# Second layer of the experts computed transposed, with the weights stationary and 496 tokens moving

## The reference, cut to what matters

```python
B, L, D = h.shape                                  # 1, 12500, 256
C = max(1, math.ceil(CAPACITY_FACTOR * T / E))     # tokens that an expert takes
buf = jnp.zeros((E, C, D), dtype=h.dtype).at[idx, pos_safe].set(x, mode='drop')
hmid = jax.nn.relu(jnp.einsum('ecd,edf->ecf', buf, w1) + b1[:, None, :])   # 256 -> 1024
ybuf = jnp.einsum('ecf,efd->ecd', hmid, w2) + b2[:, None, :]               # 1024 -> 256
y_tok = ybuf[idx, pos_g] * (prb * kept)[:, None]
y = jnp.nan_to_num(y_tok.reshape(B, L, D), nan=0.0, posinf=10000.0, neginf=-10000.0)
```

## Time and profile before

| | |
|---|---|
| median of three runs | 1618.15 us |
| the profiled execution's own time | 1620.16 us |
| its span, first to last instruction | 1618.4 us |
| TensorE busy | 1425.0 us (88%) |
| DVE busy | 1194.5 us (74%) |
| ACT busy | 929.4 us (57%) |
| POOL busy | 685.3 us (42%) |
| mean granted TensorE clock | 0.941 of full speed |

### The profile page before, as it was taken

How to read it: one execution, slowest core, us unless ns; L and a number is a source line. 1 busy time by engine, 2 the same in 40 slices (tenths; PEclk the granted TensorE clock), 3 DMA queues, 4 the chain that set the end, 5 groups by cost and what they waited for, 6 DMA issues and landing times. The chain is left out here.

```text
span 1618.4 us, 30409 instructions
## 1 busy us (share of the span) xinstructions
PE 1425.0 (88%) x8833; PEld 1261.1 (78%) x8833; DVE 1194.5 (74%) x3087; ACT 929.4 (57%) x1980; POOL 685.3 (42%) x598
## 2 busy tenths in 40 slices
PE   5999999994877777777747999999999999999995
PEld 5999999983655556566536999999999999999994
DVE  5888888874778878878754677776777677777864
ACT  3555555541445645645555676767667676766762
POOL 0000000006556556656624355455455545465434
PEclk8999999996889898989867999999999999999998
DMA  2434434422433443443611121121313112121000
GB/s 78 83 82 82 83 84 84 84 63 70 91 83 85 107 90 81 99 102 81 162 45 50 55 73 20 32 77 47 93 35 99 33 47 78 46 77 41 17 14 18
DMA packets 109592, 112.12 MB, mean 69 GB/s; under 512 B 66311, under 2 KB 89113, under 8 KB 109422
## 3 DMA queue, kind: packets, MB, share of 16 engines
q1 hardware_dynamic: 56682, 72.73, 18.1%
q0 software_dynamic: 52864, 38.82, 11.5%
HBM read 76.17 MB, written 43.85 MB: 74 GB/s over the span
## 5 line engine op out<-in xcount | busy, mean ns | idle before, releaser
L1534 DVE TENSOR_TENSOR h_lo<-q_all,h_hi 128x496 fp32r<-128x496 f32 x256 | 173.4, 677 | 197.9 <-PE psY L1595 89.1
L1332 POOL DMA_INDIRECT out<-q_all,to_i x128 | 176.1, 1376 | 327.9 <-issue 293.2
L1410 ACT ACTIVATE h_hi<-psH,b_sb 128x496 fp32r<-128x496 f32 x256 | 172.6, 674 | 233.4 <-PE psH L1618 225.7
L1595 PE MATMUL psY<-w_hi,h_hi 128*124 128x256 f32 x1024 | 289.3, 283 | 0.0
L1595 PE MATMUL psY<-w_hi,h_lo 128*124 128x256 f32 x1024 | 287.0, 280 | 0.0
L1595 PE MATMUL psY<-w_lo,h_hi 128*124 128x256 f32 x1024 | 286.7, 280 | 0.0
L748 POOL DMA_INDIRECT gl<-alpha_l_table,isrc x100 | 130.5, 1305 | 174.3 <-issue 133.6
L1595 PEld LDWEIGHTS psY<-w_lo,h_hi 128*124 128x124 f32 x1024 | 188.9, 184 | 8.9
L1595 PEld LDWEIGHTS psY<-w_hi,h_hi 128*124 128x124 f32 x1024 | 188.7, 184 | 7.9
L1595 PEld LDWEIGHTS psY<-w_hi,h_lo 128*124 128x124 f32 x1024 | 189.1, 185 | 0.0
L1319 POOL DMA_INDIRECT q_all<-out,from_i x112 | 164.7, 1471 | 54.7 <-issue 54.7
(11 more groups left out here) (230 smaller groups left out, 3338.4 us busy)
## 6 DMA issues: line engine op xcount, KB each, us to landing
x_sb<-in_x SPq DMA_DIRECT2D x50, 448.0 KB
q_all<-in_L_ffn_w SPq DMA_DIRECT2D x16, 1024.0 KB
graph_table<-tab_sb SPq DMA_DIRECT2D x25, 511.0 KB
out<-xd SPq DMA_DIRECT2D x25, 448.0 KB
x_sb<-in_x SPq DMA_DIRECT2D x50, 52.0 KB
out<-q_all,to_i POOLq DMA_INDIRECT x128
q_all<-out,from_i POOLq DMA_INDIRECT x112
gl<-alpha_l_table,isrc POOLq DMA_INDIRECT x100
```

The lines of the kernel that those rows point to most:

```text
L1332: pool.indirect_dma_start(out=out, in_=o_sb[:, par, j, :], in_offset=None, out_offset=bass.IndirectOffsetOnAxis(ap=to_i[:, par, j:j + 1], ...
L1410: act.activation(h_hi[:, f % 4, :], psH[f % 2][:, 0:TS3], ACT.Relu, bias=b1_sb[:, bass.ds(e * NF + f, 1)]).then_inc(s_hhi_ready, 1)
L1534: nc.vector.tensor_tensor(h_lo[:, f % 4, :], hf[:, f % 4, :], h_hi[:, f % 4, :].bitcast(F32), ALU.subtract).then_inc(s_hlo_ready, 1)
L1595: ins = nc.tensor.matmul(psY[par][j // 2][0:T3, (j % 2) * D:(j % 2 + 1) * D], hh[:, f % 4, j * T3:(j + 1) * T3], w[:, f, :], start=f == 0 ...
```

## The change

`second` is turned round. The stationary operand is a 128 by 128 block of `w2`, the moving one is all 496 tokens of `h_hi` or `h_lo`: three passes by two halves of the output channels, 6 matmuls in the place of 12. The result now has channels on partitions and tokens in the free dimension. So

- `with_bias` adds a bias per partition (128 partitions by 496, two instructions as before) and writes `y_t`; `b2` is loaded as rows and turned together with `b1`, in the place of a copy on all partitions;
- a new step of TensorE, `back`, turns `y_t` with eight transposes into `psX`, in step 3 of the next tile, between the first layer's matmuls and `second`; it waits for both of `with_bias`'s instructions;
- `times_prob` reads `psX` and moves from steps 2 and 3 to steps 3 and 5;
- the transposes of step 6, which write the same `psX`, wait for the end of `times_prob`;
- on DVE `limits` and `finite` move from steps 4 and 5 to 6 and 7, and `keep_finite` and `sums` from steps 6 and 7 to steps 0 and 1 of the tile after, ahead of `with_bias`;
- at the end, `keep_finite` and `sums` of the last tile but one, and a last `back`, stand in the closing sequence.

```diff
@@ -699,15 +699,15 @@
-                    b2_end, b1_end = w2_end + E * D, w2_end + E * D + P
+                    bias_end = w2_end + P
...
-                    split_dma(sp, q_all[:, 0, w2_end:b2_end].rearrange("p (a n) -> p a n", a=1),
-                              b2.rearrange("(a e) d -> a (e d)", a=1).partition_broadcast(T3), T3, s_first_in)
-                    sp.dma_start(q_all[0:E * NF, 0, b2_end:b1_end], b1.rearrange("e (c p) -> (e c) p", p=P))\
+                    sp.dma_start(q_all[0:E * NF, 0, w2_end:bias_end], b1.rearrange("e (c p) -> (e c) p", p=P))\
...
+                    sp.dma_start(q_all[E * NF:E * NF + E * KC, 0, w2_end:bias_end],
+                                 b2.rearrange("e (c p) -> (e c) p", p=P)).then_inc(s_first_in, 16)
...
@@ -1194,9 +1194,9 @@
-            b2_bc = carve(T3, E, D)
-            b1_rows = carve(E * NF, P)
-            b1_sb = sb3("b1_sb", [P, E * NF])
+            NBIAS = E * NF + E * KC
+            bias_rows = carve(NBIAS, P)
+            bias_t = sb3("bias_t", [P, NBIAS])
@@ -1210,7 +1210,7 @@
-            yb = carve(T3, J, D)
+            y_t = carve(P, KC, TS3)
...
@@ -1282,6 +1283,9 @@
+
+            def has_two_before(e, st):
+                return not (isinstance(e, int) and e == 0 and st < 2)
@@ -1391,9 +1395,11 @@
                         act.wait_ge(s_fin_done, n - 1)
-                    act.wait_ge(s_yb_done, 2 * (n - 1) + pair + 1)
+                    act.wait_ge(s_y_back, 2 * (n - 1) + pair + 1)
+                    passed(act, s_act_passed)
                     for j in range(2 * pair, 2 * pair + 2):
-                        ins = act.activation(ys[:, j, :], yb[:, j, :], ACT.Copy, scale=prob[:, bass.ds(J * (n - 1) + j, 1)])
+                        ins = act.activation(ys[:, j, :], psX[pair][0:T3, (j % 2) * D:(j % 2 + 1) * D], ACT.Copy,
+                                             scale=prob[:, bass.ds(J * (n - 1) + j, 1)])
                     ins.then_inc(s_ys_done, 1)
@@ -1408,15 +1414,15 @@
                             act.activation(h_hi[:, f % 4, :], psH[f % 2][:, 0:TS3], ACT.Relu,
-                                           bias=b1_sb[:, bass.ds(e * NF + f, 1)]).then_inc(s_hhi_ready, 1)
+                                           bias=bias_t[:, bass.ds(e * NF + f, 1)]).then_inc(s_hhi_ready, 1)
                             act.activation(hf[:, f % 4, :], psH[f % 2][:, 0:TS3], ACT.Relu,
-                                           bias=b1_sb[:, bass.ds(e * NF + f, 1)]).then_inc(s_hf_ready, 1)
+                                           bias=bias_t[:, bass.ds(e * NF + f, 1)]).then_inc(s_hf_ready, 1)
                             if is_first(e, st):
...
                                 root(g + 1)
-                            if f in (2, 3) and not is_first(e, st):
-                                times_prob(g, f - 2)
+                            if f in (3, 5) and not is_first(e, st):
+                                times_prob(g, (f - 3) // 2)
                             if f == 4 and not end:
@@ -1510,13 +1516,12 @@
                 def with_bias(n, par, e):
 
-                    dve.wait_ge(s_ys_done, 2 * (n - 1))
+                    dve.wait_ge(s_y_back, 2 * (n - 1))
                     dve.wait_ge(s_w2_mm, NF * n)
-                    for pair in range(2):
-                        nc.vector.tensor_tensor(yb[:, 2 * pair:2 * pair + 2, :],
-                                                psY[par][pair][0:T3, :].rearrange("p (j d) -> p j d", j=2),
-                                                b2_bc[:, bass.ds(e, 1), :].broadcast_to([T3, 2, D]),
-                                                ALU.add).then_inc(s_yb_done, 1)
+                    for c in range(KC):
+                        nc.vector.tensor_tensor(y_t[:, c, :], psY[par][c][:, 0:TS3],
+                                                bias_t[:, bass.ds(KC * e + E * NF + c, 1)].broadcast_to([P, TS3]),
+                                                ALU.add).then_inc(s_yt_ready, 1)
 
                 def body(e, last):
@@ -1539,16 +1544,16 @@
                             if f == 1 and not end:
                                 scales(g + 1)
-                            if f == 4 and after:
-                                limits(g)
-                            if f == 5 and after:
-                                finite(g)
+                            if f == 0 and has_two_before(e, st):
+                                keep_finite(g - 1)
+                            if f == 1 and has_two_before(e, st):
+                                sums(g - 1, par, (st - 2) % ST, e * (ST // 2) + (st - 2) // 2)
                             if f == 6 and not end:
                                 low_t(g + 1, 1 - par)
                             if f == 6 and after:
-                                keep_finite(g)
+                                limits(g)
                             if f == 7 and after:
-                                sums(g, 1 - par, (st - 1) % ST, e * (ST // 2) + (st - 1) // 2)
+                                finite(g)
                             if st == ST - 1 and not last:
                                 split_w1(f, e + 2)
@@ -1557,6 +1562,8 @@
                 over_experts(dve, body)
+                keep_finite(NG - 1)
+                sums(NG - 1, 0, ST - 2, NG // 2 - 1)
                 with_bias(NG, 1, E - 1)
@@ -1569,33 +1576,43 @@
                     pe.wait_ge(s_hit, KC * g)
                     pe.wait_ge(s_lot, KC * g)
+                    if not (isinstance(g, int) and g < 2):
+                        pe.wait_ge(s_ys_done, 2 * (g - 1))
                     for c in range(KC):
                         for j in range(J):
...
                     ins.then_inc(s_t_done, 1)
 
-                pe.wait_ge(s_first_in, 80)
-                nc.tensor.transpose(psY[0][0][:, 0:E * NF], b1_rows[:, :], ident[0:E * NF, 0:E * NF]).then_inc(s_b1_t, 1)
+                pe.wait_ge(s_first_in, 64)
+                nc.tensor.transpose(psY[0][0][:, 0:NBIAS], bias_rows[:, :], ident[0:NBIAS, 0:NBIAS]).then_inc(s_b1_t, 1)
                 transposes(0)
                 pe.wait_ge(s_b1_set, 1)
 
+                def back(n):
+
+                    pe.wait_ge(s_yt_ready, KC * n)
+                    for pair in range(2):
+                        for j in range(2 * pair, 2 * pair + 2):
+                            for c in range(KC):
+                                ins = nc.tensor.transpose(psX[pair][0:T3, (j % 2) * D + c * P:(j % 2) * D + (c + 1) * P],
+                                                          y_t[:, c, j * T3:(j + 1) * T3], ident[:, :])
+                        ins.then_inc(s_y_back, 1)
+
                 def second(e, st, f):
 
                     g, par = ST * e + st, st % 2
                     if f == 0 and not (isinstance(e, int) and e == 0 and st < 2):
-                        pe.wait_ge(s_yb_done, 2 * (g - 1))
+                        pe.wait_ge(s_yt_ready, KC * (g - 1))
                     if st == 0:
                         pe.wait_ge(s_w2hi, NF * e + f + 1)
...
                     pe.wait_ge(s_hhi_ready, NF * g + f + 1)
                     pe.wait_ge(s_hlo_ready, NF * g + f + 1)
-                    for j in range(J):
-                        for n, (hh, w) in enumerate(((h_hi, w2_hi), (h_hi, w2_lo), (h_lo, w2_hi))):
-                            ins = nc.tensor.matmul(psY[par][j // 2][0:T3, (j % 2) * D:(j % 2 + 1) * D],
-                                                   hh[:, f % 4, j * T3:(j + 1) * T3], w[:, f, :],
-                                                   start=f == 0 and n == 0 and j % 2 == 0,
-                                                   stop=f == NF - 1 and n == 2 and j % 2 == 1)
+                    for n, (w, hh) in enumerate(((w2_hi, h_hi), (w2_lo, h_hi), (w2_hi, h_lo))):
+                        for c in range(KC):
+                            ins = nc.tensor.matmul(psY[par][c][:, 0:TS3], w[:, f, c * P:(c + 1) * P], hh[:, f % 4, :],
+                                                   start=f == 0 and n == 0, stop=f == NF - 1 and n == 2)
                     ins.then_inc(s_w2_mm, 1)
 
@@ -1621,6 +1638,8 @@
                                 transposes(g + 1)
+                            if f == 3 and not is_first(e, st):
+                                back(g)
                             if f >= 2:
@@ -1629,6 +1648,7 @@
                 for f in range(NF - 2, NF):
                     second(E - 1, ST - 1, f)
+                back(NG)
 
         late.close()
 

```

13 lines of the change are left out of this document (7 added, 6 removed).

## The result

The changed kernel takes 1679.07 us, the median of four runs (1674.64 to 1681.53); the kernel before took 1617.85 us beside it (1615.28 to 1619.96). The ratio is 1.0376, with a 95% interval of 1.0349 to 1.0403: slower by 61 us, where 67 were forecast. The profiled execution took 1674.64 us, its span is 1672.6 us.

The account below looks back on a forecast made before the run. TensorE, without idle time at full clock, was taken as the bound. -18 + 24.8 + 44 + 11.5 + 3.4 = 66 us on the profiled 1620.16 gave 1686, 1684 against the median, written as 1685 us; range 1665 to 1710.

Parts of the forecast that it names:

- Parts 1 and 2: TensorE's queue: six matmuls of `second` for twelve save 18 us; `back`'s eight transposes add 24.8 us in 31 tiles.
- part 1: `second` on TensorE takes 1.34 us for 1.41, 0.07 us less, 256 times: 18 us saved.
- Part 3: `back` on TensorE waits for DVE's `with_bias`, 1.0, 1.7 or 2.5 us in 29 tiles: together 44 us.
- Part 4: Step 6's transposes wait for ACT's `times_prob`: 0.24 us in 23 tiles, 0.86 in 7; together 11.5 us.
- Part 5: Closing sequence: `with_bias` comes 1.9 us later on DVE, ACT then starts 1.5 us later; sum 3.4 us.
- at nothing: Priced at zero: `with_bias` itself, loads of `b2`, POOL's gathers (rows used over a tile later), the later limits.
- The queue alone: Rival: both new waits of TensorE are met in time, only its queue and the end count; 1628 us, chance 0.09.
- The not slower case: Rival: `back`'s transposes cost half of 0.77 us per block, waits are met; 1615 or 1616 us, chance 0.03.
- The clock rival: Rival: waits lower TensorE's clock, 3 us lost in 7 first tiles of experts: 1706 us, or above 1730; chance 0.12.

Follow-up runs that it names:

- Experiment 11: The kernel of experiment 3 with POOL's gathers issued ahead of the scatter: 1632.86 us, ratio 1.0081.
- experiment 6: The kernel of experiment 5 with every transpose of `back` made twice, sixteen per tile in the place of eight: 1675.91 us, ratio 1.0362.
- Experiment 1: The changed kernel with `back` writing into the PSUM bank of its own result, where `times_prob` reads it: 1677.69 us, ratio 1.0357.
- experiment 9: The changed kernel with POOL's gathers issued ahead of the scatter: 1681.51 us, ratio 1.0376.
- experiment 3: Experiment 1 with `back` moved to step 4, `normal` to 3 and `times_prob` to 4 and 5: 1647.14 us, ratio 1.0159.
- experiment 2: The changed kernel with `sums` moved from step 1 to step 2, behind `with_bias` and `h_lo`: 1695.99 us, ratio 1.0463.
- 10: The kernel of experiment 2 with POOL's gathers issued ahead of the scatter: 1650.8 us, ratio 1.0206.
- 4: The kernel before with the changed kernel's order on DVE alone, nothing transposed: 1637.89 us, ratio 1.0113.
- 5: The changed kernel with DVE's order of the kernel before and both pairs of `times_prob` in step 3: 1649.14 us, ratio 1.0190.
- 7: The kernel of experiment 5 with `y_t` and the identity as fp32r, so `back` transposes in that type; the text gives no run time.
- 12: The kernel of experiment 3 with DVE's order of the kernel before: 1663.42 us, ratio 1.0280.

## Why the prediction was right, and what in it was not

**The mechanism held.** Both new waits are there, at the lines and in the tiles named, `with_bias` follows `sums` without a gap, and the tiles come in the forecast order: 24.2 and 24.4 us for the ordinary ones (24.4 forecast), 25.5 and 25.6 for the two others (25.7 and 25.9 forecast). Experiment 11 against the changed kernel prices the waits together at 46 us (1679.07 - 1632.86), and leaves 14.5 for queue and end.

**Parts 1 and 2** gave 18 us less for `second` and 24.8 more for `back`; counted by starts, 14.3 and 26.2 came, so the queue costs 11.9 us, not 6.8. The term that was mis-sized is `back`. A step of `second` that doesn't stand behind transposes takes 1.345 us on average where it took 1.416, which is the 0.07 of part 1. But the first pair of matmuls behind transposes takes 0.08 us longer (experiment 6), and the count by starts books that to `second`. With it `back` costs 0.87 us, and 0.93 behind a wait, and not 0.80. The rows of before had it too: the first matmul behind the transposes at 1202.37 is shown with 0.37 us where 0.28 is usual. In the prediction I set the rule of the Trainium skill, "TensorE: Matmul & The Clock Gate", part 2, against this; eight transposes by its 0.45 us would have made experiment 6 cost 14 us, and it cost 26.8. The same section calls that rule one for a matmul by itself and gives 81 ns for each of a stream of loads and matmuls of 128 columns. By that eight would take 0.65 us, an estimate from the page, and experiment 6 would cost 20 us. It is nearer, and still too low for fp32; the trace was the better source.

**Part 3** gave 44 us, 34.3 came, and it is the largest error of a term. Two things were mis-sized, by about as much. One is the hand-over: I took 0.19 us of ACT to DVE for DVE to TensorE, and `back` starts 0.05 us after the adds in every tile in which it waits. That is 0.14 us in 29 tiles, 4 of the 9.7 us. 0.05 had been the lower bound. The other is the chain on DVE: 1.99 us were added in the tile shown and not 2.15. 0.70 us in the ordinary tile is 1.0 less 0.14 less 0.16. In an expert's last tile the chain was 0.2 us too long, in the first tile of the next nearly 0.4.

**Part 4** gave 11.5 us, 8.3 came: 0.10 to 0.18 us in an ordinary tile and 0.75 in an expert's last. The pair of `times_prob` took 0.83 us and not 0.90, and ACT's hand-over to TensorE 0.14 us and not 0.19:

```profile
1196.82 0.83 ACT L1401 ACTIVATE q_all<-psX,prob 124x256 f32<-124x256 f32 x2
...
1197.79 1.04 PE L1583 MATMUL psX<-ident,q_all 124*128 124x124 f32 x8
```

Experiment 1 shows that this term wasn't additive: of its 8.3 us, 5.6 come back ahead of `back` in the first tiles of the experts. **Part 5** gave 3.4 us and 3.4 came, from the last `h_lo` to the end. The waits were forecast 13 us too long and the queue 5 us too short, so the sum, 66, is 8 us over the 57.9. That the measured median is 61, nearer still to the forecast, is luck.

**What failed is a cost "at nothing".** I let POOL's gathers go free because their rows are used more than a tile later and `sums` moves by only 5 us. From the end of `sums` to the statistics there were some 24 to 25 us before and up to 18.4 are needed; the new order leaves one tile less 5 us, about 19. In the changed kernel that just holds, as TensorE's waits have made its tile 24.2 us and more: experiment 9 moves the gathers 6.6 us ahead and gains nothing. But it is the next limit, at some 24 us a tile. Whoever removes TensorE's waits alone gets 1647 us (experiment 3) in the place of 1633 (11), without a fall of the clock in either, and whoever shortens DVE's chain gets 1696 (2) in the place of 1651 (10). The forecast of the time didn't suffer; the main forecasts of experiments 2, 3 and 4 did.

**The rivals.** The queue alone (1628) needed waits met in time: they weren't, and experiment 11 shows that this case would have been 1633. The not slower case needed `back` below 0.47 us; experiment 6 excludes it, and even as fp32r it takes 0.62. The clock rival needs more care. In the profiled execution of the changed kernel the clock stayed at 1.00 from 900 to 1550 us, with gaps of 0.7 to 2.0 us in every tile. But in the profiled executions of seven experiments it fell to 0.50 for some three us at a time: once in 1, six times in 2, three in 5, two in 6, one in 7, two in 9 and three in 12. Each fall began within 1.7 us of the end of a wait of TensorE of 2.0 to 3.0 us. The changed kernel and these seven have 53 such waits, of 1.9 us or more, and 18 falls; the kernels whose longest wait in this block was 1.4 us or less had none. So the rival's path exists, at 1.6 us a fall and not the 3 that it was priced at, and it begins with the waits of the changed kernel's first tiles (experiment 9). Whether the changed kernel's three other executions, 3 to 7 us slower than the profiled one, had such falls isn't shown. The same page of the Trainium skill, part 1, says that short pauses between groups of matmuls can make the clock swing; the traces agree for waits of 2 us and more, and the shorter ones of these runs did nothing. Its other warning, of idle gaps longer than any here, would have let none of the falls come.

**Left open.** What in DVE's chain at the change of experts is 0.4 us shorter than I reckoned; why gathered rows are taken up 1.3 us after the last issue in some tiles and 3.4 in most; and why only some waits of 2 to 3 us are followed by a fall of the clock.

## What to carry to other kernels

When a result that goes through one more engine is wanted by the engine that never waits, count what the other engines have queued ahead of it, and price the hand-over by several rows between the same two engines. An instruction that is moved later on its engine also moves everything that its completion releases: follow it round (here `sums`, scatter, gather, `stats`, `sums`) and compare the length of the ring with the time of a tile, before it is called free. A wait that is removed shows its worth only when the next ring is open too: the same edit of `sums` cost 17 us with the ring closed (experiment 2, some 10 of them by the clock) and saved 31 with it open (10 against 9). And a mean clock of 0.99 or 1.00 over 650 us can hide a fall that costs 1.6 us; look at the stretches behind the longest waits.
